# Maxima subtracted from attention scores: four matmuls of 512 columns a job in place of sixteen of 128

## The chip, the cores and the metric

The kernel runs on one core of a Trainium2 chip. The time is device time in microseconds (us) for one launch, as the median of several runs. The engines are named as in the profile: PE is TensorE's matmul array and PEld its weight loads, DVE is VectorE, ACT is ScalarE, POOL is GpSimd and SP is SyncE.

## The reference

Four transformer blocks work in turn on x (16 samples, 128 tokens, 128 channels). There are five attentions with 16 heads of 8 channels each: over the 128 tokens and then over the sample's context of 77 in the first block, over the context in the second, over the tokens and then the context in the third. The last block has one attention over the context without heads, then experts and a gate. What the change touches is the softmax of the attentions with heads. Cut to that:

```python
def mha(q, k, v):                      # q: 128 tokens, k and v: 128 or 77 tokens, 16 heads of 8
    scores = jnp.einsum('bqhd,bkhd->bhqk', qh, kh) / jnp.sqrt(d)
    attn = jax.nn.softmax(scores, axis=-1)
    out = jnp.einsum('bhqk,bkhd->bqhd', attn, vh)
    return out.reshape(B, Nq, C)
```

The softmax takes each row's maximum away before the exponential. The maximum belongs to a query and a head.

## The kernel before

The 16 samples go in four groups of four. An attention of one sample is a job; there are 5 x 16 = 80, numbered in the order in which they run. Each engine works through an order written out by hand (PE_ORDER, DVE_ORDER, ACT_ORDER, POOL_ORDER), and semaphores join them. In the orders, `s:j:g` is a score product of job j, `mx:j:g` its row maxima, `tu:j` and `tr:j` the turn of the maxima of jobs j and j+1, `st:j` the transposed score product, `su:j` the subtract, `ex:j:half` the exponentials, `av:j` the product with the values and `t1:j` its unloading.

The 128 channels lie on 128 partitions, so four strips of 32 partitions hold four heads each (strip g, head hh of the strip). A job runs as follows:

- `scores` (L1098, L1101, L1107, L1109): for each strip, queries on partitions and four heads' keys in a row of 512 or 308 columns, into one of the four banks of the PSUM tile ring. A bank is used by the next item but three, whatever it is, once the reader has freed it.
- `maximum` (L849, DVE): the maxima over the keys, four columns of mhl for each strip. Two jobs share one mhl: job j of a pair writes columns 32g + 4(j % 2) to +3.
- `turn` (L1145, PE, and L858, DVE), once for two jobs: mhl is transposed into a ring bank and copied to the tile mt, where row 32g + 4(j % 2) + hh has the maxima of that head by query.
- `scores_t` (L1128, L1133, L1137, PE): the same scores with the keys on partitions, into the PSUM tile big, one bank for each strip: 512 columns, four heads of 128 queries. It stays open for accumulation.
- `subtract` (L1154, PE): adds minus the maximum to each column of big. Each matmul works on one strip's 32 rows. The weights are a slice of indb, -1 in the row of the wanted head and job and 0 in the other 31 rows, for all kw key columns; the moving operand is the strip of mt, 128 columns. Four heads times four strips make 16 matmuls.
- ACT then takes the exponentials of big in two halves (L637, strips 0 and 1, then 2 and 3) into P, and frees big; PE multiplies P with the values (L1170).

On PE the subtract of an even job stands behind the turn in the order, often with `st` between (`tu:22 st:22 su:22`), at times with little or nothing (`tu:6 av:5 su:6`, `tu:20 s:22:1 su:20`). The subtract waits for the bank of the turn to be freed, which the copy L858 does. On DVE the copy stands among the row maxima of later jobs and among unloadings, as in `mx:22:0 tr:20 mx:22:1`.

The tile indb is made once at the start (`first_masks`): sel8 is summed from the identity, one column for each of the eight rows 4(j % 2) + hh that a strip uses, and indb is its negative, spread over 128 columns (L748).

Of the kernel before, what the change touches and what calls it, by code (L numbers as in the profile page):

```python
# [8 lines left out]
BF16 = mybir.dt.bfloat16  # L9
U8 = mybir.dt.uint8  # L10
ACT = mybir.ActivationFunctionType
ALU = mybir.AluOpType
AX = mybir.AxisListType.X

B, T, D, C = 16, 128, 128, 77
# [238 lines left out]
def job_of(j):  # L254
    return ORDER[j // GB] + (j % GB,)


def pair_of(j):

    return j - j % 2  # L260
# [25 lines left out]
def build(nc, x_in, ctx_in, ctxT_in, condT_in, ws_in, w_in, col_in, vcol_in, row_in, rw_in, rb_in, gb_in, mqk_in, mkq_in,  # L286
          mc_in, cos_in, sin_in, ident_in, ind_in, onesp_in, out):
    ctx = ExitStack()
    with ctx:
        def sb(name, shape, dt=F32):  # L290
            return ctx.enter_context(nc.sbuf_tensor(name, shape, dt))

        def ps(name, shape, dt=F32):
            return ctx.enter_context(nc.psum_tensor(name, shape, dt))
# [6 lines left out]
        big = ps("big", [128, 4, 512])  # L301
# [18 lines left out]
        oneb = sb("oneb", [128, 512], BF16)  # L320
        hm4 = sb("hm4", [128, 4])
        sel8 = sb("sel8", [128, 8])
        indb = sb("indb", [128, 8, 128], BF16)
        mqk8 = sb("mqk8", [128, 4, T], U8)
        mkq8 = sb("mkq8", [128, 4, T], U8)
        mc8 = sb("mc8", [128, B * C], U8)
# [42 lines left out]
        kbm = sb("kbm", [128, 2, 4, 128], BF16)  # L369
        P = sb("P", [128, 2, H, T])  # L370
        mhl = sb("mhl", [128, 2, 128], BF16)
        mt = sb("mt", [128, 2, 128], BF16)
        avt = [sb(f"avt{i}", [128, 2, GB * 128]) for i in range(2)]
        avm = [sb(f"avm{i}", [128, GB * 128]) for i in range(2)]
        rv = [sb(f"rv{i}", [128, 2, 16, 2]) for i in range(2)]
# [41 lines left out]
        def bank(item):  # L417
            return RING[item] % NB

        def full(eng, item):  # L420

            eng.wait_ge(ring_full[bank(item)], RING[item] // NB + 1)

        def taken(eng, item):

            eng.wait_ge(ring_free[bank(item)], RING[item] // NB + 1)

        def at(item, p=128):
            return ring[0:p, bank(item), :]

        def free(item):
            return ring_free[bank(item)]
# [267 lines left out]
        def _(dve):  # L700
            v = nc.vector
            n_setup = [0]

            def chain(i):
                n_setup[0] += 1
                i.then_inc(setup_dve, 1)
                dve.wait_ge(setup_dve, n_setup[0])
# [36 lines left out]
            def first_masks():  # L744
                dve.wait_ge(ident_ld, 16)
                v.tensor_copy(identb[:], ident[:])
                chain(v.tensor_reduce(sel8[:], ident[:].rearrange("p (g c) -> p c g", c=32)[:, 0:8, :], AX, ALU.add))
                v.tensor_scalar(indb[:], sel8[:].unsqueeze(2).broadcast_to([128, 8, 128]), -1.0, None, ALU.mult)  # L748
                dve.wait_ge(consts_in, 16 * 8)
                v.tensor_scalar(mqk[:], mqk8[:], -1.0, BIG, ALU.add, ALU.mult)  # L750
                v.tensor_scalar(mkq[:], mkq8[:], -1.0, BIG, ALU.add, ALU.mult).then_inc(masks_ready, 1)
# [30 lines left out]
            def statistics(k, s):  # L782
                t, o = (C, 1) if k == 4 else (128, 0)
                n, turn = s + NS * o, 1 if k == 4 else LN_TURN[k]
                src = ctx_t[s] if k == 4 else xs[s]
                if k == 4:
                    dve.wait_ge(ctx_in_s[s], 32)
                elif k == 0:
                    dve.wait_ge(x_in_s[s], 16)
                elif k in (5, 7):  # L790
                    taken(dve, ("o2" if k == 5 else "o4", "y", s))
                    hold(dve)
                else:
                    dve.wait_ge(x_ready[s], x_turn({1: "o0", 2: "o1", 3: "m0", 6: "o3", 8: "m1"}[k]))
                    hold(dve)
                for b in range(GB):
                    i = v.bn_stats(bst[s][0:t, o, b, :], src[0:t, b, :])
                i.then_inc(ln_bn[n], 1)
                dve.wait_ge(ln_bn[n], turn)
                for b in range(GB):  # L800
                    i = v.bn_aggr(mv[s][0:t, o, b, :], bst[s][0:t, o, b, :])  # L801
                i.then_inc(ln_stats[n], 1)
# [49 lines left out]
            def turn(j):  # L852
                item = ("tu", j)
                if j >= 4:

                    dve.wait_ge(st_full, 2 * (j - 3) + 2)
                full(dve, item)
                v.tensor_copy(mt[:, j // 2 % 2, :], at(item).bitcast(BF16)[:, 0:T]).then_inc(free(item), 1)  # L858

            def unload(j):  # L860
                item, p, b = ("av", j), j // GB, j % GB
# [102 lines left out]
            for item in DVE_ORDER:  # L964
                st, part, *_ = item
                if st == "mx":
                    maximum(part, item[2])
                elif st == "tr":
                    turn(part)
                elif st == "t1":  # L970
                    unload(part)
                elif st == "nr":
                    invert(part)
                elif st == "nt":
                    turn_back(part)
                elif st == "first":
                    (first_tables, first_weights, first_masks)[part]()
                elif st == "u":
                    unit(part)
                elif part == "stat":  # L980
                    statistics(int(st[1:]), item[2])
                elif part == "qc":
                    cast(int(st[1:]), item[2])
                elif st == "p0" and part in ("q", "k"):
                    roped(item[2], part)
                elif st == "p0" and part != "v":
                    rope(item[2], part)
                elif st[0] == "p":
                    values(int(st[1:]), item[2])
                elif st == "x3":  # L990
                    mixture(item[2], part)
                else:
                    add_result(st, item[2])

        @block.tensor
        def _(pe):
            mm = nc.tensor.matmul
# [10 lines left out]
            for c in range(2):  # L1008
                i = mm(big[:, 0, c * B:(c + 1) * B], WS[:, MODS[c][0], :], condT[:], start=True, stop=True)
# [137 lines left out]
            def subtract(j):  # L1147
                kw = ATT[job_of(j)[0]]["kw"]
                taken(pe, ("tu", pair_of(j)))
                for half in range(2):  # L1150
                    for hh in range(4):
                        for g in (2 * half, 2 * half + 1):
                            r = slice(32 * g, 32 * g + 32)
                            i = mm(big[0:kw, g, hh * T:(hh + 1) * T], indb[r, 4 * (j % 2) + hh, 0:kw], mt[r, j // 2 % 2, :], start=False,  # L1154
                                   stop=(hh == 3), skip_group_check=True)
                    i.then_inc(st_full, 1)

            def av(j):
# [142 lines left out]
            for item in PE_ORDER:  # L1301
                st, part, *_ = item
                if st == "s":
                    scores(part, item[2])
                elif st == "st":
                    scores_t(part)
                elif st == "tu":
                    turn(part)
                elif st == "su":
                    subtract(part)  # L1310
                elif st == "av":
                    av(part)
                elif st == "u":
                    unit(part)
                elif st == "f":
                    fold(part)
                elif part == "t":
                    norm(int(st[1:]), item[2])
                elif st[0] == "p":
                    project(int(st[1:]), item[2], part)  # L1320
                elif st[0] == "o":
                    outproj(int(st[1:]), item[2])
                elif st[0] == "m":
                    mlp(int(st[1:]), item[2], part)
                else:
                    mixture(item[2], part)
# [93 lines left out]
```

## Time and profile before

| | |
|---|---|
| median of 3 runs | 591.42 us (589.92 to 594.17) |
| the profiled execution | 592.24 us, its span 590.2 us |
| granted clock of TensorE in the profile, mean | 0.967 |
| PE busy | 553.6 us, 94% |
| DVE busy | 377.0 us, 64% |
| ACT busy | 311.6 us, 53% |
| POOL busy | 341.8 us, 58% |

The span is the time from the first to the last instruction; the time of the execution is longer by 2.0 us. Busy times are what an engine spent in instructions, overlaps counted once. A matmul that is recorded takes from its start to the arrival of its last column, and the next one starts before that; weight loads (PEld) overlap matmuls too. In the timeline, neighbours of one kind are merged into a row with the start of the first, the time until the end of the last and their number.

### The profile page before, as it was taken

What the parts mean: (1) busy time and instruction counts of PE and PEld (TensorE: products, weight loads), DVE (VectorE), ACT (ScalarE), POOL (GpSimd) and SP (SyncE); (2) the same over time, 40 slices, a digit from 0 to 9 for tenths busy, and PEclk for the clock granted to TensorE, in tenths of its full rate; (3) what the DMA queues carried; (4) which work ended last, traced back from release to release, by engine and by line L of the source; (5) the groups of instructions that cost most, each with busy time, mean ns of one, the idle gap of its engine ahead of it and who ended that gap; (6) DMA issues with size and microseconds to landing.
All of it is one profiled execution on the core that took longest, in us unless ns stands there. A gap on an engine that the chain in (4) does not pass through costs nothing. (4 is left out here: it accounts for less than half of the span.)

```text
span 590.2 us, 17700 instructions
## 1 busy us (share of the span) xinstructions
PE 553.6 (94%) x7235; PEld 346.6 (59%) x7260; DVE 377.0 (64%) x1034; ACT 311.6 (53%) x515; POOL 341.8 (58%) x428
## 2 busy tenths in 40 slices
PE   4899999899989999999999999999999999998996
PEld 1524455456545665566565655665577756866475
DVE  3567878975887468956795669888548404424024
ACT  1013365356445846766657565645846565535561
POOL 6365877486687768868746858779738103322000
PEclk8758999999999999999999999999999999998999
DMA  7800200000100010001000100000000000000000
GB/s 272 306 7 4 74 21 3 21 20 9 29 4 21 3 37 2 21 3 37 3 21 2 37 3 3 2 19 4 19 2 3 1 1 2 18 19 1 0 1 36
DMA packets 16574, 16.06 MB, mean 27 GB/s; under 512 B 3090, under 2 KB 14620, under 8 KB 16240
## 3 DMA queue, kind: packets, MB, share of 16 engines
q1 hardware_dynamic: 15632, 10.82, 6.0%
q10 hardware_dynamic: 864, 4.13, 1.8%
q8 instruction: 58, 0.95, 0.7%
q14 instruction: 20, 0.16, 0.1%
HBM read 13.85 MB, written 1.09 MB: 25 GB/s over the span
## 5 line engine op out<-in xcount | busy, mean ns | idle before, releaser
L637 ACT ACTIVATE P<-big 77x1024 f32<-77x1024 f32 (+1 forms) x160 | 155.2, 1018 | 130.9 <-PE big L1154 129.8
L849 DVE TENSOR_REDUCE mhl<-ring 128x4 bf16<-128x308 f32 (+1 forms) x320 | 164.4, 547 | 40.2 <-PE ring L1109 29.4
L564 POOL TENSOR_TENSOR qm<-qT,hm 128x512 f32<-128x512 f32 x80 | 85.1, 1068 | 36.6 <-PE big L1154 16.4
L536 POOL TENSOR_SCALAR xn<-x,mv,rstd 128x128 f32<-128x128 f32 x128 | 103.6, 821 | 3.3
L551 POOL TENSOR_TENSOR kbm<-kT,hm 128x308 bf16<-128x308 f32 (+1 forms) x80 | 68.5, 859 | 46.0 <-PE ring L1109 24.7
L1137 PE MATMUL big<-qm,kT 32*77 32x512 f32 (+1 forms) x640 | 92.1, 621 | 0.9 <-ACT P L637 0.8
L1029 PE MATMUL ring<-hT,W 128*128 128x512 f32 x176 | 91.9, 622 | 0.9 <-ACT hT L621 0.2
L1170 PE MATMUL ring<-P,Vp 77*32 77x128 f32 (+1 forms) x2560 | 86.6, 276 | 3.6 <-DVE mhl L849 1.4
L1170 PEld LDWEIGHTS ring<-P,Vp 77*32 77x32 f32 (+1 forms) x2560 | 65.4, 109 | 21.9 <-issue 13.1
L530 POOL TENSOR_SCALAR rstd<-mv 128x4 f32<-128x4 f32 (+1 forms) x36 | 9.7, 268 | 87.6 <-DVE mv L801 84.3
L621 ACT ACTIVATE hT<-ring,tab 128x128 f32<-128x128 f32 x96 | 35.9, 458 | 45.3 <-PE ring L1051 45.0
L1041 PEld LDWEIGHTS ring<-W,hid 128*128 128x128 f32 x480 | 57.4, 192 | 3.5 <-issue 2.6
L1041 PE MATMUL ring<-W,hid 128*128 128x128 f32 x480 | 57.5, 275 | 0.0
L1109 PE MATMUL ring<-kbm,qb 32*128 32x308 bf16 (+1 forms) x256 | 53.7, 317 | 3.6 <-issue 1.1
L1154 PEld LDWEIGHTS big<-mt,indb 32*77 32x77 bf16 (+1 forms) x1280 | 33.9, 104 | 31.7 <-issue 23.2
L866 DVE STREAM_TRANSPOSE avt<-ring 128x256 f32<-128x256 f32 x80 | 35.3, 442 | 21.6 <-PE ring L1170 20.8
L1029 PEld LDWEIGHTS ring<-hT,W 128*128 128x128 f32 x176 | 30.0, 193 | 29.1 <-issue 22.1
L670 ACT ACTIVATE hid<-ring,tab 128x128 f32<-128x128 f32 x112 | 31.4, 375 | 22.3 <-PE ring L1029 22.2
L532 POOL TENSOR_TENSOR rstd<-rstd,mhalf 128x4 f32<-128x4 f32 (+1 forms) x36 | 38.2, 1062 | 3.0
L1154 PE MATMUL big<-mt,indb 32*77 32x128 bf16 (+1 forms) x1280 | 39.2, 218 | 0.4
L575 POOL TENSOR_TENSOR avm<-avt,rv 128x256 f32<-128x256 f32 x40 | 24.5, 632 | 18.5 <-DVE rv L873 17.0
L1109 PEld LDWEIGHTS ring<-kbm,qb 32*128 32x128 bf16 x256 | 16.8, 92 | 28.5 <-issue 20.5
(164 smaller groups left out, 740.4 us busy)
## 6 DMA issues: line engine op xcount, KB each, us to landing
gring<-gate_rows SPq DMA_DIRECT2D x20, 256.0 KB, 3.4
W<-in_w ACTq DMA_DIRECT2D x1, 2624.0 KB, 14.4
hid<-in_ws SPq DMA_DIRECT2D x1, 1536.0 KB, 14.6
x<-in_x SPq DMA_DIRECT2D x4, 256.0 KB, 7.4
out<-x SPq DMA_DIRECT2D x4, 256.0 KB, 2.0
W<-in_w ACTq DMA_DIRECT2D x1, 768.0 KB, 4.8
ctxT<-in_ctxT SPq DMA_DIRECT2D x4, 154.0 KB
ctx<-in_ctx SPq DMA_DIRECT2D x4, 154.0 KB
```

The source lines that it names most:

```text
L532: nc.gpsimd.tensor_tensor(rstd[s][0:t, o, 1, :], rstd[s][0:t, o, 0, :], mhalf[0:t, :], ALU.pow).then_inc(ln_rstd[n], 1)
L536: i = nc.gpsimd.tensor_scalar(dst[0:t, b, :], src[0:t, b, :], mv[s][0:t, o, b, 0:1], rstd[s][0:t, o, 1, b:b + 1], ALU.subtract, ALU.mult)
L551: nc.gpsimd.tensor_tensor(kbm[:, j % 2, :, 0:kw], k.broadcast_to([128, 4, kw]), mask.broadcast_to([128, 4, kw]), ALU.mult).then_inc(kbm_re ...
L564: nc.gpsimd.tensor_tensor(qm[:, j % 2], q.broadcast_to([128, 4, T]), mask.broadcast_to([128, 4, T]), ALU.mult).then_inc(qm_ready, 1)
L637: nc.scalar.activation(P[0:kw, j % 2, 8 * half:8 * half + 8, :], big[0:kw, 2 * half:2 * half + 2, :].rearrange("p g (h q) -> p (g h) q", h=4),
L849: v.tensor_reduce(mhl[:, j // 2 % 2, c:c + 4], at(item)[:, 0:4 * kw].rearrange("p (h k) -> p h k", h=4), AX, ALU.max).then_inc(free(item), 1)
L1029: i = mm(at(item, m)[:, 0:n], w, a, start=(c == 0), stop=(c == len(parts) - 1))
L1041: i = mm(o[:, b * 128:(b + 1) * 128], a[:, b * t:(b + 1) * t], w, start=(c == 0 and bias is None), stop=(c == len(wts) - 1), skip_group_ch ...
L1109: give(item, mm(o, qb[s][r, b * T:(b + 1) * T], k_, start=(a > 1), stop=True, skip_group_check=True))
L1137: mm(big[0:kw, g, :].rearrange("p (h q) -> p h q", h=4), kT[s][r, b * kw:(b + 1) * kw], qm[r, j % 2], start=(a > 1), stop=False, skip_grou ...
L1154: i = mm(big[0:kw, g, hh * T:(hh + 1) * T], indb[r, 4 * (j % 2) + hh, 0:kw], mt[r, j // 2 % 2, :], start=False, stop=(hh == 3), skip_group ...
L1170: i_ = mm(at(item)[32 * g:32 * g + 32, i * T:(i + 1) * T], Vp[(j // GB) % 2][0:kw, b, h, :], P[0:kw, j % 2, h, :], start=(t == 0), stop=(t ...
```

## The change

The tile mt gets four times the columns: one part of 128 for each head hh, in which only the rows of head hh (of either job of the pair) have the maxima and all other rows are 0. DVE writes it with one multiply of the ring bank, read four times over, with head4, a column of ones and zeros for each head (`128 x 4`, spread over the queries). indb shrinks to one slice for each job of the pair, with -1 in that job's four rows of each strip. A subtract is then one matmul of 512 columns for each strip. In the setup, head4 and job2 are summed from sel8. The orders of all engines are as before, and so are the waits.

```diff
-        indb = sb("indb", [128, 8, 128], BF16)
+        indb = sb("indb", [128, 2, 128], BF16)
+        head4 = sb("head4", [128, 4])
+        job2 = sb("job2", [128, 2])
...
-        mt = sb("mt", [128, 2, 128], BF16)
+        mt = sb("mt", [128, 2, 4, T], BF16)
...
-                v.tensor_scalar(indb[:], sel8[:].unsqueeze(2).broadcast_to([128, 8, 128]), -1.0, None, ALU.mult)
+                v.tensor_tensor(head4[:], sel8[:, 0:4], sel8[:, 4:8], ALU.add)
+                chain(v.tensor_reduce(job2[:], sel8[:].rearrange("p (j h) -> p j h", j=2), AX, ALU.add))
+                v.tensor_scalar(indb[:], job2[:].unsqueeze(2).broadcast_to([128, 2, 128]), -1.0, None, ALU.mult)
...
-                v.tensor_copy(mt[:, j // 2 % 2, :], at(item).bitcast(BF16)[:, 0:T]).then_inc(free(item), 1)
+                v.tensor_tensor(mt[:, j // 2 % 2], at(item).bitcast(BF16)[:, 0:T].unsqueeze(1).broadcast_to([128, 4, T]),
+                                head4[:].unsqueeze(2).broadcast_to([128, 4, T]), ALU.mult).then_inc(free(item), 1)
...
                 for half in range(2):
-                    for hh in range(4):
-                        for g in (2 * half, 2 * half + 1):
-                            r = slice(32 * g, 32 * g + 32)
-                            i = mm(big[0:kw, g, hh * T:(hh + 1) * T], indb[r, 4 * (j % 2) + hh, 0:kw], mt[r, j // 2 % 2, :], start=False,
-                                   stop=(hh == 3), skip_group_check=True)
+                    for g in (2 * half, 2 * half + 1):
+                        r = slice(32 * g, 32 * g + 32)
+                        i = mm(big[0:kw, g, :].rearrange("p (h q) -> p h q", h=4), indb[r, j % 2, 0:kw], mt[r, j // 2 % 2],
+                               start=False, stop=True, skip_group_check=True)
                     i.then_inc(st_full, 1)
```

## Rows read from the trace of the kernel before

**Rows 1.** The page, part 1: busy time, share of the span, instructions.
```profile
PE 553.6 (94%) x7235; PEld 346.6 (59%) x7260; DVE 377.0 (64%) x1034; ACT 311.6 (53%) x515; POOL 341.8 (58%) x428
```
**Rows 2.** Waits, longest first: engine, line, releaser, us in total, times, longest.
```profile
ACT P L637 <- PE big L1154: 129.8, 63, 8.6
...
PEld big L1154 <- DVE mt L858: 5.2, 13, 0.9
...
PEld ring L1098 <- DVE mhl L849: 2.4, 3, 1.4
...
PEld ring L1041 <- DVE mhl L849: 1.8, 4, 1.1
```
**Rows 3.** Stages: start:end, length, busy us of PE, PEld, DVE, ACT, POOL; clock.
```profile
40.00:100.00 60.00, 56.51 (x922) 28.86 (x920) 46.50 (x117) 25.82 (x39) 43.13 (x52) 0.92 0.09 25
...
340.00:400.00 60.00, 56.84 (x978) 36.21 (x983) 50.49 (x128) 35.68 (x45) 43.98 (x53) 1.00 0.03 7
```
**Rows 4.** Groups by form (busy us, mean ns, idle before); the last: min/median/max ns.
```profile
L1109 PE MATMUL ring<-kbm,qb 32*128 32x308 bf16 x192 | 36.2, 296 | 1.6 <-issue 0.9 <-DVE mhl L849 0.7
L1109 PE MATMUL ring<-kbm,qb 32*128 32x512 bf16 x64 | 17.7, 382 | 2.0 <-POOL kbm L551 1.0 <-POOL qm L564 0.7 <-issue 0.3
L840 DVE CAST qb<-qT 128x512 bf16<-128x512 f32 x20 | 10.9, 543 | 10.4 <-ACT qT L607 10.0
L890 DVE TENSOR_TENSOR oT<-ring,gring 128x512 f32<-128x512 f32 x20 | 13.7, 687 | 18.7 <-PE ring L1041 18.7
L824 DVE TENSOR_TENSOR kT<-ring,cosT 128x512 f32<-128x512 f32 x4 | 2.8, 692 | 8.3 <-PE ring L1029 8.2
L858 DVE COPY mt<-ring 128x128 bf16<-128x128 bf16 x40 | 8.5, 212 | 11.6 <-PE ring L1145 11.4
L1154 PE MATMUL big<-mt,indb x1280: 212/214/309, 44.0 to 472.4; 32*77 32x128 bf16 x110, 32*128 32x128 bf16 x73
```
**Rows 5.** Timeline at a plain subtract, job 2: start, us, engine, line, operation.
```profile
55.86 1.14 PE L1137 MATMUL big<-qm,kT 32*128 32x512 f32 x8
56.82 0.41 PE L1154 MATMUL big<-mt,indb 32*128 32x128 bf16 x16
57.16 1.05 PE L1041 MATMUL ring<-W,hT 128*128 128x128 f32 x7
```
**Rows 6.** Timeline of PE where 512-column score matmuls precede a full-height item.
```profile
240.22 0.80 PE L1109 MATMUL ring<-kbm,qb 32*128 32x512 bf16 x3
240.95 0.54 PE L1170 MATMUL ring<-P,Vp 77*32 77x128 f32 x12
```
**Rows 7.** Stages, instructions of the tile mt alone (PE, PEld, DVE).
```profile
340.00:400.00 60.00, 7.81 (x240) 7.04 (x240) 1.51 (x7) 1.00 0.03 7
...
sum 440.00, PE 39.21 PEld 33.86 DVE 8.49; mean PE 4.90 PEld 4.23 DVE 1.06
```
**Rows 8.** Timeline of PE at a mixed subtract, job 40.
```profile
268.13 0.21 PE L1154 MATMUL big<-mt,indb 32*77 32x128 bf16 x1
...
268.58 0.26 PE L1154 MATMUL big<-mt,indb 32*77 32x128 bf16 x3
```
**Rows 9.** Timeline of a pair with margin, jobs 24 and 25.
```profile
178.62 0.23 DVE L858 COPY mt<-ring 128x128 bf16<-128x128 bf16 x1 [0.73 <-PE ring L1145]
...
180.16 0.41 PE L1154 MATMUL big<-mt,indb 32*128 32x128 bf16 x16
```
**Rows 10.** Timeline of a pair without margin, jobs 20 and 21.
```profile
162.98 0.22 DVE L858 COPY mt<-ring 128x128 bf16<-128x128 bf16 x1
...
163.25 0.29 PEld L1154 LDWEIGHTS big<-mt,indb 32*77 32x77 bf16 x16 [0.36 <-DVE mt L858]
```
**Rows 11.** Timeline where a score product waits for a row maximum.
```profile
117.04 0.10 PEld L1098 LDWEIGHTS ring<-mqk,identb 32*32 32x32 bf16 x4 [0.73 <-DVE mhl L849]
```
**Rows 12.** Timeline of DVE in the setup.
```profile
8.30 0.69 DVE L748 TENSOR_SCALAR indb<-sel 128x1024 bf16<-128x1024 f32 x1
11.79 0.43 DVE L750 TENSOR_SCALAR mqk<-mqk 128x512 bf16<-128x512 uint8 x1 [2.80 <-DMA mkq<-in_mkq]
```

## The prediction

> **What bounds the kernel now.** I read the busy times first. The array (PE) is busy for 553.6 of 590.2 us, 94%; VectorE (DVE) for 377.0, 64% [rows 1]. PE's own waits are short: the longest in total are a few microseconds, and none of the larger ones is at the subtract (L1154) [rows 2]. So the order of the array's work sets the time, and the change is worth what it takes from the array's path or puts on it. By stage the picture holds: PE is busy for 56.5 of 60 us between 40 and 100 and for 56.8 between 340 and 400, VectorE for 46.5 and 50.5; the second of these is its fullest stage [rows 3]. ScalarE waits for the subtract for 129.8 us in all, in 63 pieces [rows 2]. That is no bottleneck, but it says that whatever makes a subtract late makes ScalarE's exponentials late as well.
>
> **Part 1, the matmuls.** A job's subtract is 16 matmuls of 128 columns now and 4 of 512 after: the same columns. What matters is how long the array is held. A single 128-column matmul has 0.214 us [rows 4], yet all 16 together take 0.41 us from the first start to the last end, and the next item, a full-height projection, starts 0.34 us after the first of them [rows 5]. The 16 starts thus lie within 0.41 - 0.214 = 0.20 us. What a column costs comes from L1109: its 512-column form takes 382 ns and its 308-column form 296 ns, so 86 ns for 204 columns, 0.42 ns each [rows 4]. 128 columns are then 0.054 us of streaming and 512 are 0.215. Sixteen starts in 0.20 us are three steps of 0.054 between four groups of four: the four strips of 32 rows already work side by side, although the program names strips 0 and 1 in the first half and 2 and 3 in the second. The strips hold 4 x 0.054 = 0.215 us each, and four matmuls of 512 columns, one in each strip, hold them for 0.215 as well. The streaming gains nothing.
>
> What of the hand-over to the next item? After the last 128-column start (57.02) the next item starts at 57.16, so 0.14 us, of which 0.054 is streaming and 0.09 a gap [rows 5]. After the last of three 512-column matmuls with 32 rows (240.22 + 0.80 - 0.39 = 240.63) a full-height item starts at 240.95, 0.32 us, of which 0.215 is streaming and 0.10 the same gap [rows 6]. After the change: some 0.02 for four starts, plus 0.32, makes 0.34, against 0.34 before. A plain subtract gains 0.
>
> Not all are plain. The busy time of the subtract's matmuls is 39.21 us over the eight stages that hold all 80 jobs [rows 7], 0.49 us a job, against 0.41 for the plain one. In the others score matmuls (L1107, L1109) come between: at 268.13 the 16 run until 268.84, some 0.71 us, with several score matmuls among them [rows 8]. Most of that is the scores' own streaming in the same strip, which stays. Upper bound of the gain: all of it goes, 80 x (0.49 - 0.40) = 7 us, 0.40 being one 512-column matmul of 0.382 plus the spread of 0.02. Lower bound: 0. I take **2 us gained**, nearer to the plain case, since about 0.06 us in each of some thirty mixed jobs can be weight loads left uncovered between the small matmuls. The 960 weight loads that go lie under matmuls in the plain case and are counted in this.
>
> A rule of the Trainium skill speaks for a larger gain. The page "TensorE: Matmul & The Clock Gate", section "Part 3: Packing small matmuls — row/col tiling", says that matmuls start and end in strict program order, whatever strip they use. By that rule strips 2 and 3 could start only after the first half, the 16 would need about 8 steps and the change would save about 0.2 us a job. The trace does not agree: 16 starts in 0.20 us leave no room for eight steps of 0.054 [rows 5].
>
> **Part 2, the tile on VectorE.** The copy of 128x128 to mt (L858), 0.212 us on average [rows 4], becomes a multiply of 128x512 from the ring bank with the head mask. It isn't in the trace. The nearest rows are the multiplies of 128x512 from the ring with a tile in SBUF: L890 at 687 ns and L824 at 692 ns; a cast of 512 elements within SBUF takes 543 ns [rows 4]. I take 0.69 (the same operation from the same memory), the cast as the low bound. So a turn costs 0.48 us more, 40 x 0.48 = 19 us of VectorE's time in all. Two places must be priced: who waits for mt, and who waits for what is queued behind it on VectorE.
>
> Who waits for mt: the subtract of the even job of each pair, on PE, with everything queued behind it there. I went through the 40 pairs in the timeline and took, for each, the time from the end of the copy to the first subtract matmul, less the 0.055 us that the signal takes at the shortest. In 27 pairs the margin is over 0.48 us, because the large score product (L1137, 0.96 us from its first start to the subtract [rows 5]) or more lies between: a copy ends at 178.85 and its subtract starts at 180.16 [rows 9]. In 13 it is less, from nothing (the copy ends at 163.20, the subtract starts at 163.25 [rows 10]) up to 0.46. The list of waits has the same number: 13 waits of the subtract's weight load for the copy, 5.2 us in all [rows 2]. The margins of the 13 add up to 2.0 us, so the loss is 13 x 0.48 - 2.0 = **4.2 us**. The odd jobs use the same mt a whole job later and have margin.
>
> Who waits for what is behind it: the row maxima (L849), which free the ring banks that PE takes next. PE waits for them today for a few microseconds in all: 2.4 + 1.8 us are the largest entries [rows 2]. At 117.04, for one, a score product starts 0.73 us late because of a maximum [rows 11]. Where VectorE then has a gap, the 0.48 us vanish in it; where it runs through, they are handed on. Bounds: 0, and one delay of 0.48 for each of the 27 pairs that don't already wait, 13 us. Following VectorE from each copy to its next gaps, and looking who takes a freed bank within the delay, I find some ten places with 0.3 us each. I take **3 us**. The odd price, the wait of L858 for its own ring item, does not change.
>
> **Part 3, the setup.** indb is written with 256 elements in place of 1024 (L748, 0.69 us) and two small operations are added. Behind them VectorE waits 2.80 us for the masks to arrive [rows 12]. That wait is the cover for either sign: 0. Without it the part would gain at most half a microsecond.
>
> **Sum**, against the profiled execution of 592.24 us (span 590.2 and 2.0 around it): -2 + 4.2 + 3 = +5.2 us. Not all of a stall on PE reaches the end: PE idles for 36.6 us of its span, places where a delay can be lost. That is 6%, and the idle places stand where the chains cross, so I keep about four fifths, **+4 us: 596**. The median of the runs shown is 591.42, 0.8 us below the profiled one. I stay on the profiled scale and forecast 596, with 592 to 600 as this case's own range.
>
> **Rivals.** (a) *VectorE becomes the bound of its full stretches.* In 340 to 400 us seven turns [rows 7] add 3.4 us to 50.49 of 60 [rows 3]. If VectorE's queue is what PE follows there and in like stretches, the delays don't die in gaps. It decides from the point where a pair's idle time on VectorE is under 0.48. Price at its worst: 4.2 + 13 lost and 0 to 2 gained, so 607 to 609; in part, from 600 up. For it: 84% busy there. Against it: PE's waits for VectorE are small today. (b) *The longer tile is covered.* Only the bare waits (the 8 pairs of the 13 with under 0.15 us of margin, 0.4 us together) grow, by 8 x 0.48 - 0.4 = 3.4 us, the banks cost nothing, and the mixed jobs give back 3: 592.6. The wait list speaks for it, the fullness of VectorE against it. (c) *The array does gain.* Either the two halves run one after the other, 4 x 0.054 = 0.2 us saved in each of 80 jobs, 16 us less (chance 0.03), or the mixed jobs give the full 7 and the gap before the next item closes because its weights load under the long matmuls, 80 x 0.09 = 7 more (chance 0.07). With the 7 of losses: 592.2 + 7 - 14 to 16, 583 to 585.5. Against it: [rows 5] for the first, and [rows 6] for the second, where the gap stands after 512 columns too. The first of the two is what the order rule of the Trainium skill's page named above would give. (d) *The change does nothing* but swap equal work, with neither stalls nor gains: also 592, and taken with (b).
>
> **How the numbers follow.** Forecast (592 to 600) 0.48; (a) 0.22; (b) with (d) (588 to 592.5) 0.20; (c) 0.10. The range leaves out the worst half of (a) and (c): 587 to 603. A difference of 1%, 5.9 us, is about what a measurement of this kernel can tell from none; against 591.4 it is reached at 597.3 and at 585.5. The forecast's upper third and all of (a) lie above: 0.16 + 0.20 = 0.36 slower; faster 0.10; same 0.54.
>
> **What the profile of the changed kernel would show.** The new multiply at about 0.69 us x40. The subtract's four matmuls within some 0.4 us and the next full-height item 0.34 us after the first: if 0.25 or less, the gap closed and (c) has a part. PE's waits for mt up from 5.2 us to about 10, in more pairs than 13. Waits of PE for L849 up by some 3 us; if by over 8, (a). PE's busy time nearly unchanged. The prediction is wrong if the multiply takes under 0.4 us, if a plain subtract holds the array for clearly less than 0.34, or if VectorE's delay is passed on in the full stretches.

## The result and the profile after

| | before | changed |
|---|---|---|
| median of the runs | 593.22 us (588.32 to 597.23, 20 runs) | 597.59 us (591.39 to 601.16, 20 runs) |
| the profiled execution | 592.24 us, span 590.2 | 591.71 us, span 589.6 |
| granted clock in it, mean | 0.967 | 0.982 |

The changed kernel is slower: the ratio of the times is 1.0065, with a 95% interval from 1.0038 to 1.0092. (Ratios leave out executions over 1.5% above the fastest of the same kernel, like the 601.16 here; medians and ranges hold them all.) Yet its profiled execution is 0.5 us *shorter* than the one of before. This has to be cleared up first. The page of the changed kernel, part 1:

```profile
PE 548.4 (93%) x6275; PEld 326.1 (55%) x6300; DVE 391.9 (66%) x1036; ACT 312.4 (53%) x515; POOL 341.5 (58%) x428
```

The stages at the start, of before (start:end, length, busy us of PE, PEld, DVE, ACT, POOL, clock):

```profile
26.20:33.00 6.80, 4.77 (x54) 2.11 (x55) 5.30 (x37) 0.00 (x0) 6.59 (x8) 0.50 0.41 110
33.00:50.00 17.00, 15.54 (x125) 3.75 (x124) 9.74 (x17) 4.72 (x7) 7.44 (x9) 0.50 0.00 1
```

The same of the changed kernel:

```profile
26.10:32.90 6.80, 5.08 (x55) 2.31 (x56) 5.31 (x37) 0.00 (x0) 6.49 (x8) 0.50 0.42 118
32.90:50.00 17.10, 16.10 (x218) 6.04 (x221) 14.88 (x31) 6.67 (x9) 11.03 (x13) 1.00 0.01 2
```

In both executions the granted clock is at its lower level (0.50, 1.2 GHz) around 26 to 33 us. In the one of before it stays there until 50; in the other it is back at the upper level (2.4 GHz) from 32.9. In the same 17 us the array gets through 218 matmuls in place of 125. That the change did not make this difference is seen from a second profile of the changed kernel ("changed, again" below). There the clock was low from 24.5 to 31.3 us and once more in this stage:

```profile
34.70:48.40 13.70, 12.62 (x102) 3.09 (x94) 8.53 (x14) 1.94 (x2) 5.42 (x7) 0.50 0.01 1
```

Its subtract of job 5 starts at 73.3 us, as in before (73.9), and not at 68.4 as in the first profile of the same kernel. So a profiled execution starts with a head start or a handicap of several microseconds. The 20 runs of the changed kernel have mean clocks from 0.961 to 0.982, and the six that are at 0.982, like the profiled one, took 591.4 to 592.8 us, the others 595.6 to 601.2.

The change has to be read from a stretch without such a piece. I take the one from the first subtract matmul of job 5 to that of job 77. It has its ends at the same work in every kernel. Differences are taken from the starts of these matmuls; the stages below have the same ends rounded to 0.1 us. Before:

```profile
73.90:455.40 381.50, 366.11 (x5739) 228.65 (x5755) 283.55 (x737) 226.79 (x320) 275.34 (x342) 1.00 0.05 13
```

The same stretch of the changed kernel:

```profile
68.40:454.70 386.30, 366.31 (x4875) 211.50 (x4891) 297.22 (x737) 227.47 (x320) 275.43 (x342) 1.00 0.05 13
```

The clock is 1.00 throughout in both. The stretch takes **4.8 us more** (386.3 - 381.5), about 0.8% of the whole, which is what the ratio of the runs says. PE's busy time in it is the same within 0.2 us, though this sum is only good to some microseconds: a kernel below with before's matmuls has 22 records more of them in this stretch. So the array does as much work as before and stands longer. VectorE is busy 13.7 us longer. The stretch starts at 73.9 and at 68.4: these 5.5 us, which lie in the clock at the start, covered the loss in the profile.

The parts. Groups of instructions (busy us, mean ns, idle before), the subtract's matmuls of before first, then two of the changed kernel:

```profile
L1154 PE MATMUL big<-mt,indb 32*77 32x128 bf16 (+1 forms) x1280 | 39.2, 218 | 0.4
L1160 PE MATMUL big<-mt,indb 32*77 32x512 bf16 (+1 forms) x320 | 39.1, 380 | 3.3 <-DVE mt L864 3.2
L864 DVE TENSOR_TENSOR mt<-ring,head 128x512 bf16<-128x512 bf16 x40 | 27.2, 680 | 11.6 <-PE ring L1152 11.4
```

The changed kernel's list of waits:

```profile
ACT P L639 <- PE big L1160: 125.8, 64, 5.2
PEld big L1160 <- DVE mt L864: 13.8, 20, 1.6
PEld ring L1116 <- DVE mhl L854: 3.4, 9, 0.9
PEld ring L1116 <- DVE mt L864: 1.0, 3, 0.4
```

Its timeline at a plain subtract, job 4, and at the pair of jobs 20 and 21:

```profile
64.61 0.39 PE L1160 MATMUL big<-mt,indb 32*128 32x512 bf16 x4
64.93 0.38 PE L1048 MATMUL ring<-W,oT 128*128 128x128 f32 x1
...
157.89 0.69 DVE L864 TENSOR_TENSOR mt<-ring,head 128x512 bf16<-128x512 bf16 x1
158.50 0.47 DVE L854 TENSOR_REDUCE mhl<-ring 128x4 bf16<-128x308 f32 x1
158.64 0.12 PEld L1160 LDWEIGHTS big<-mt,indb 32*77 32x77 bf16 x4 [0.83 <-DVE mt L864]
```

Four matmuls of 512 columns hold the array for 0.32 us until the next full-height item, where sixteen of 128 held it for 0.34 [rows 5]. The busy time of the subtract's matmuls is 39.1 us as it was [rows 7]. The multiply takes 0.680 us in place of 0.212 [rows 4]. At jobs 20 and 21 the array stands until the multiply ends (157.89 + 0.69 = 158.58, first weight load at 158.64), as it did for the copy [rows 10]. The subtract's weight loads now wait for mt 20 times and for 13.8 us, where it was 13 times and 5.2 [rows 2]. The array itself idles 3.3 us before the subtract's matmuls, 3.2 of it for mt, where it was 0.4 in all. Waits for row maxima grow as well, over all lines: those of the weight loads from 7.8 to 10.6 us, those of the array from 5.9 to 7.1. And three score products now wait for the multiply, 1.0 us together; before had no such wait.

### The profile page after: what moved, and what is told of

The parts are those of the page before. It is cut to its first block and busy times, and to the rows that moved or that the text cites. A ratio compares the mean times of both kernels' runs of the same rounds, so it can differ in the third digit from the quotient of the medians.

```text
span 589.6 us, 15782 instructions
## 1 busy us (share of the span) xinstructions
PE 548.4 (93%) x6275; PEld 326.1 (55%) x6300; DVE 391.9 (66%) x1036; ACT 312.4 (53%) x515; POOL 341.5 (58%) x428
## 5 line engine op out<-in xcount | busy, mean ns | idle before, releaser
L1160 PE MATMUL big<-mt,indb 32*77 32x512 bf16 (+1 forms) x320 | 39.1, 380 | 3.3 <-DVE mt L864 3.2
L577 POOL TENSOR_TENSOR avm<-avt,rv 128x256 f32<-128x256 f32 x40 | 24.5, 632 | 20.6 <-DVE rv L880 19.0
L1116 PEld LDWEIGHTS ring<-kbm,qb 32*128 32x128 bf16 x256 | 17.1, 92 | 33.6 <-issue 22.7
L864 DVE TENSOR_TENSOR mt<-ring,head 128x512 bf16<-128x512 bf16 x40 | 27.2, 680 | 11.6 <-PE ring L1152 11.4
## 6 DMA issues: line engine op xcount, KB each, us to landing
W<-in_w ACTq DMA_DIRECT2D x1, 2624.0 KB, 14.9
```

Source lines behind the costliest of these rows:

```text
L1116: give(item, mm(o, qb[s][r, b * T:(b + 1) * T], k_, start=(a > 1), stop=True, skip_group_check=True))
L1160: i = mm(big[0:kw, g, :].rearrange("p (h q) -> p h q", h=4), indb[r, j % 2, 0:kw], mt[r, j // 2 % 2], start=False, stop=True, skip_group_c ...
```

## The experiments

Each kernel was timed beside the kernel before on the same chip. Since the clock pieces move whole runs by several microseconds, the table also has the stretch from job 5 to job 77, and the later part of it from job 41 to 77, each as the difference to before (381.5 and 182.2 us). "Clock" is what pieces at the lower level the stretch held.

| kernel | ratio, 95% interval | 5 to 77 | 41 to 77 | clock |
|---|---|---|---|---|
| changed kernel | 1.0065 [1.0038, 1.0092] | +4.8 | +2.0 | none |
| changed, again | 1.0135 [1.0088, 1.0182] | +4.8 | +2.0 | none |
| wide tile alone | 1.0180 [1.0129, 1.0231] | +7.4 | +3.6 | none |
| four matmuls alone | 0.9983 [0.9952, 1.0014] | -1.4 | -1.2 | none |
| delay behind the copy, multiply | 1.0258 [1.0210, 1.0306] | +13.3 | +3.3 | 17.1 us |
| delay behind the copy, reduce | 1.0076 [1.0041, 1.0112] | +3.8 | +1.9 | none |
| changed, subtracts later | 1.0167 [1.0112, 1.0222] | +18.9 | +2.0 | 2 x 17.1 us |
| before, subtracts later | 1.0139 [1.0071, 1.0206] | +10.5 | 0.0 | 17.1 us |
| two heads at a time | 1.0051 [1.0016, 1.0087] | +0.3 | -0.1 | none |
| multiply twice | 1.0463 [1.0418, 1.0508] | +30.5 | +12.0 | 6.8 and 3.4 us |
| half-wide tile alone | 1.0036 [0.9979, 1.0093] | +3.1 | +0.9 | 3.4 us |
| before, three subtracts later | 1.0039 [0.9989, 1.0089] | +3.1 | +0.2 | 2 x 3.4 us |

The second line is the changed kernel once more, timed together with the next three kernels. Its ratio is twice as far from 1 as the first one, and the two intervals barely touch, while its stretch is the same within 0.03 us. Before with nine or with three subtracts later has before's own time from job 45 to job 77 (within 0.04 us of 164.2), too. For differences under 1% the stretch is therefore the better evidence. It leaves out what happens outside it: the kernel with two heads at a time is 0.5% slower by its runs and the same by the stretch.

The expectations count to job 79 (398.3 us before). I end at job 77, because in three kernels (wide tile alone, delay with the reduce, three subtracts later) a short piece at the lower clock lies between the two. Where an expectation names a time, the time to job 79 is given beside it.

> The changed kernel itself, for its time on the same chip as the three others: 3 to 6 us slower than before, and 403 us between the subtracts of jobs 5 and 79.

To job 79 it took 403.1 us, as expected; its runs were 7.5 us above before's, not 3 to 6 (597.46 us, 592.68 to 599.93, 6 runs, beside 589.97).

### The wide tile alone

```diff
+                    for hh in range(4):
+                        for g in (2 * half, 2 * half + 1):
+                            r = slice(32 * g, 32 * g + 32)
+                            i = mm(big[0:kw, g, hh * T:(hh + 1) * T], indb[r, j % 2, 0:kw], mt[r, j // 2 % 2, hh, :], start=False,
+                                   stop=(hh == 3), skip_group_check=True)
```

> VectorE's part of the change alone: mt is written 512 columns wide by the multiply with the head mask, and the subtract stays at 16 matmuls of 128 columns. My theory puts the whole loss here: the turn is 0.47 us longer, the 13 bare subtracts and the freed banks cost 4 to 7 us against before, and the run is as slow as the changed kernel or up to 2 us slower; between the first plain subtract of a full-clock stretch (job 5) and the last (job 79), 398.3 us before, it takes 403 to 405. The rival, that four wide matmuls cost the array something of their own, expects this run at before's time.

It ran in 599.73 us (597.73 to 646.14, 6 runs) beside 589.97. Its stages for the stretch, and its waits:

```profile
69.20:458.10 388.90, 369.00 (x5742) 228.07 (x5759) 297.99 (x737) 227.53 (x320) 276.24 (x342) 1.00 0.05 13
```
```profile
PEld big L1161 <- DVE mt L864: 13.4, 20, 1.4
```

388.9 - 381.5 = 7.4 us lost: the wide tile costs more than the whole change. To job 79 it is 406.4 us, more than the 403 to 405 expected. The waits for mt are those of the changed kernel, and the array's own idle time for mt is 2.8 us. The change's matmuls beside this tile are worth 4.8 - 7.4 = -2.6 us.

### The four matmuls alone

Each strip's matmul reads the 128 columns of the copied mt four times over, with the weights of one head. It adds a wrong head's maximum to three quarters of the scores, and the exponentials get a smaller scale so that they stay finite; the work is otherwise that of before.

```diff
+                        i = mm(big[0:kw, g, :].rearrange("p (h q) -> p h q", h=4), indb[r, 4 * (j % 2), 0:kw],
+                               mt[r, j // 2 % 2, :].unsqueeze(1).broadcast_to([32, 4, T]), start=False, stop=True,
+                               skip_group_check=True)
```

> TensorE's part alone: mt is copied 128 columns wide as before, and the subtract is four matmuls of 512 columns that read mt's strip four times over. The computation differs in two places: all four heads of a strip get the maxima of the first one, and the exponential is scaled down by 0.001 so that nothing overflows. My theory: 16 small matmuls already ran four side by side, so 0 to 3 us are gained against before, and a plain subtract is followed by the next full-height item after 0.32 us against 0.34. The rival (the array gains by fewer matmuls) expects 7 to 16 us less.

It ran in 588.96 us (585.19 to 594.18, 12 runs). Stages for the stretch, waits, and the timeline at a plain subtract:

```profile
71.40:451.60 380.20, 363.89 (x4876) 211.85 (x4891) 283.64 (x737) 227.11 (x320) 276.28 (x342) 1.00 0.05 13
```
```profile
PEld big L1153 <- DVE mt L858: 5.9, 13, 0.9
```
```profile
67.64 0.39 PE L1153 MATMUL big<-mt,indb 32*128 32x512 bf16 x4
67.96 1.16 PE L1041 MATMUL ring<-W,oT 128*128 128x128 f32 x8
```

The starts of the matmuls are 380.1 us apart, against 381.5: 1.4 us gained, over 72 jobs 0.02 us each, which is the difference of the plain case (0.32 against 0.34). The waits for mt stay at 13. So the array gains little, whatever VectorE does.

### The delay behind the copy alone

To tell those who wait for mt from those who wait for what is queued behind it, the copy stays as it was, and an idle operation stands behind it. mt is ready as before; VectorE is later for the rest. First with a multiply of 312 columns:

```diff
+        pad = sb("pad", [128, 312])
...
                 v.tensor_copy(mt[:, j // 2 % 2, :], at(item).bitcast(BF16)[:, 0:T]).then_inc(free(item), 1)
+                v.tensor_tensor(pad[:].rearrange("p (a b) -> p a b", a=3), onesf[:, 0:104].unsqueeze(1).broadcast_to([128, 3, 104]),
+                                onesf[:, 0:104].unsqueeze(1).broadcast_to([128, 3, 104]), ALU.mult)
```

> The kernel before with an idle operation of 312 elements (about 0.48 us) on VectorE right behind the copy to mt, so that mt and the ring bank are ready as early as before and only what is queued behind is late. It separates the two prices of the longer turn. By the sum of the prediction: 3 us slower than before, with PE's waits for the copy as before (13, about 5 us). The rival, that the delay of the queue is the main price, expects 5 us or more; a rival by which it dies in gaps expects 0 to 1.

It ran in 605.4 us (601.37 to 610.48, 6 runs). It does not measure the queue alone. Its idle operation took 0.626 us on average (statistics of its line below, min/median/max), and the clock was at 0.50 from 102.5 to 119.6:

```profile
L860 DVE TENSOR_TENSOR pad<-onesf x40: 458/474/1349, 40.6 to 469.7; 128x312 f32<-128x312 f32 x40
```

What stretched the operation stands in the trace. The longest one, with GpSimd's operations around it:

```profile
181.57 1.04 POOL L565 TENSOR_TENSOR qm<-qT,hm 128x512 f32<-128x512 f32 x1
181.60 1.35 DVE L860 TENSOR_TENSOR pad<-onesf 128x312 f32<-128x312 f32 x1
182.57 1.28 POOL L552 TENSOR_TENSOR kbm<-kT,hm 128x512 bf16<-128x512 f32 x1
```

It ends at 182.95, 0.34 us after the qm that was running when it started (181.57 + 1.04 = 182.61). Of the 14 idle operations over 0.6 us, 12 start while a two-operand operation of GpSimd (qm, kbm or avm) is running, and each of the 12 ends 0.33 to 0.35 us after it. All that ran with GpSimd idle took 0.46 to 0.47. The kbm that starts inside it takes 1.28 us, where the same one takes 1.04 in the run with the reduce below. So this delay is longer than meant in 14 places, and it delays GpSimd too.

The 13.3 us divide at job 17: 6.5 up to there, with the piece at the lower clock, and 6.8 from there to job 77 with the clock at 1.00, as much as the wide tile costs in that part (6.7). They are not the price of a queue that is 0.47 us late. The delay was repeated with a reduce of one operand:

```diff
+        pad = sb("pad", [128, 3])
...
+                v.tensor_reduce(pad[:], onesf[:, 0:104].unsqueeze(1).broadcast_to([128, 3, 104]), AX, ALU.max)
```

> The kernel before with an idle reduction over 312 elements of one SBUF tile (about 0.47 us, one operand) behind the copy to mt. In the earlier run of this kind the idle operation read SBUF twice and took 0.63 us on average, up to 1.35, so it overstated the delay. If the queue's price is 3 us as in the prediction's sum, the stretch between the subtracts of jobs 5 and 79 takes 401 to 402 us; if the queue is the main price of the wide tile (8.1 us in that stretch in all), 404 or more; if it dies in gaps, 398 to 399.

596.97 us (593.48 to 598.27, 10 runs). Stages for the stretch, waits, and the timeline of VectorE around the turn of jobs 20 and 21:

```profile
69.20:454.50 385.30, 372.10 (x5761) 229.00 (x5756) 294.93 (x773) 227.23 (x320) 275.14 (x342) 1.00 0.05 13
```
```profile
PEld big L1156 <- DVE mt L859: 6.3, 15, 0.9
PEld ring L1111 <- DVE mhl L850: 2.7, 7, 0.9
```
```profile
158.50 0.22 DVE L859 COPY mt<-ring 128x128 bf16<-128x128 bf16 x1
158.64 0.47 DVE L860 TENSOR_REDUCE pad<-onesf 128x3 f32<-128x312 f32 x1
159.03 0.85 DVE L850 TENSOR_REDUCE mhl<-ring 128x4 bf16<-128x308 f32 x2
```

385.3 - 381.5 = 3.8 us lost, with the waits for mt nearly as before, and with no idle time of the array for mt. To job 79 it is 402.6 us, between the 401 to 402 of the prediction's sum and the 404 of its rival. So about half of the wide tile's price is the queue behind it. The delay is slightly smaller than the tile's: here the next row maximum starts 0.53 us after the copy's start (158.50 to 159.03), of which the copy's own share is 0.14 (to 158.64); in the changed kernel it starts 0.61 after the multiply's (157.89 to 158.50). In proportion (0.61 - 0.14 = 0.47 to 0.53 - 0.14 = 0.39) the queue's part would be up to 4.6 us, an estimate. What is left of the 7.4 is 2.8 to 3.6. This is a difference of two runs: it holds the waits for mt, the three waits of a score product for the multiply, and whatever the two prices do to each other.

### Covering the waits: subtracts later in PE's order

In nine jobs whose subtract stands bare behind the turn, the subtract and the item behind it change places, in the changed kernel and in the one before.

```diff
+LATER = (6, 10, 20, 22, 28, 30, 36, 46, 62)
+for _j in LATER:
+    _k = PE_ORDER.index(("su", _j))
+    PE_ORDER[_k], PE_ORDER[_k + 1] = PE_ORDER[_k + 1], PE_ORDER[_k]
```

> The changed kernel with the subtracts of jobs 6, 10, 20, 22, 28, 30, 36, 46 and 62 one item later in PE's order, so that the longer turn of these pairs is covered. If the bare waits for mt cost 4 us, some 3 of them come back and the stretch from job 5 to 79 takes 400 to 401 us in place of 403.1; if the main price lies in the queue, it stays at 402.5 to 403.5.

> The same nine subtracts one item later in the kernel before. There the copy costs 0.21 us and seven of the nine are bare or nearly so, with 0.2 to 0.9 us of standing each: 1 to 2 us less than before in the stretch (396.5 to 397.5) if that standing is real, no change if it is only moved on to ScalarE's exponentials.

Both were slower than what they started from: 602.47 us (596.3 to 603.76, 6 runs) and 600.7 (595.85 to 604.85, 6 runs), to job 79 417.2 and 408.8 us. The waits for mt did shrink. In the changed kernel with the swaps, and in before with them:

```profile
PEld big L1165 <- DVE mt L869: 7.3, 14, 0.8
```
```profile
PEld big L1159 <- DVE mt L863: 2.1, 7, 0.4
```

13.8 us became 7.3, and 5.2 became 2.1. From job 41 on, where the clock is at 1.00 and jobs 46 and 62 have moved, nothing is gained all the same: +2.0 with or without the swaps in the changed kernel, 0.0 in before. The next score products stand behind the row maxima of the same VectorE queue. I read this as the stall only changing its name; no run takes both waits away at once.

The loss is early. In before with the swaps 1.4 us are gone by job 17, at the upper clock throughout, where the subtracts of jobs 6 and 10 have moved. The timeline at job 22 and the stages after it:

```profile
173.21 0.44 PE L1159 MATMUL big<-mt,indb 32*77 32x128 bf16 x16
...
173.78 1.04 POOL L569 TENSOR_TENSOR qm<-qT,hm 128x512 f32<-128x512 f32 x1 [1.17 <-PE big L1159]
174.77 1.04 POOL L556 TENSOR_TENSOR kbm<-kT,hm 128x512 bf16<-128x512 f32 x1
...
175.87 0.60 PE L1103 MATMUL ring<-mqk,identb 32*32 32x512 bf16 x4 [1.41 <-POOL kbm L556]
```
```profile
175.90:193.00 17.10, 17.10 (x205) 10.31 (x205) 7.75 (x21) 4.96 (x8) 6.30 (x8) 0.50 0.06 18
```

GpSimd's next qm waited 1.17 us for the later subtract, and kbm stands behind it in GpSimd's order. PE in turn waited 1.41 us for kbm, and right behind that wait the clock is at 0.50 for 17.1 us, with PE busy all the time. From job 17 to job 26, which holds both the wait and this piece, 7.6 us are lost; another 1.3 go between jobs 26 and 32, at the upper clock. The changed kernel with the swaps has the same piece at 176.1, and another of 17.1 us at 101.0; the other eleven profiles have none between 123 and 282 us. So the piece comes with the swaps. That the wait of 1.41 us brought it is likely, but no run takes away that wait alone.

The last three swaps alone (jobs 36, 46 and 62), on before:

> The kernel before with only the subtracts of jobs 36, 46 and 62 one item later. In the run with nine moved ones the clock fell at 175.9 us, after an idle stretch behind the moved subtract of job 22; this leaves that out. If the bare waits for mt are worth their length, the stretch is 0.3 to 0.7 us shorter than before; if the banks that the same VectorE queue frees are the next thing late, it is unchanged within 0.1.

595.19 us (590.84 to 596.72, 8 runs), ratio 1.0039, to job 79 402.1 us. From job 45 to 77, where jobs 46 and 62 have moved, the difference is 0.0: nothing is gained. Of the 3.1 us that its stretch lost, 2.7 lie before job 17, where its order is still that of before. There it has two pieces of 3.4 us at the lower clock, at 103.9 and 117.6, which no swap explains.

### How the price grows with the turn

Three kernels change the length of the turn. The half-wide tile has two copies of the maxima (heads of even and of odd number) and takes 0.412 us; in the first kernel eight matmuls of 256 columns use it, in the second the sixteen of before. The third writes the wide tile twice, once to a buffer that nobody reads.

```diff
-        mt = sb("mt", [128, 2, 4, T], BF16)
+        mt = sb("mt", [128, 2, 2, T], BF16)
...
+                    for m in range(2):
...
+                            i = mm(big[0:kw, g, 256 * m:256 * m + 256].rearrange("p (h q) -> p h q", h=2), indb[r, 2 * (j % 2) + m, 0:kw],
+                                   mt[r, j // 2 % 2], start=False, stop=(m == 1), skip_group_check=True)
```

> Half the change: mt 256 columns wide (two masks, by the parity of the head) and eight matmuls of 256. The multiply should take about 0.42 us (0.21 more than the copy, against 0.47 for the full change). My theory has the loss grow with the length of the turn and only part of the pairs exposed: 8.1 us for 0.47 more would be 2.5 to 3.5 for 0.21, less about 1 gained on the array, so 400 to 401 us in the stretch. The rival, that any multiply in place of the copy costs the same, expects 403.

594.11 us (590.58 to 598.73, 12 runs). Groups and waits:

```profile
L864 DVE TENSOR_TENSOR mt<-ring,head 128x256 bf16<-128x256 bf16 x40 | 16.5, 412 | 12.1 <-PE ring L1152 11.9
```
```profile
PEld big L1161 <- DVE mt L864: 8.5, 16, 1.3
```

The stretch differs from before by +0.3 us (398.6 us to job 79, where 400 to 401 was expected): the matmuls' gain and the tile's price cancel.

```diff
+                v.tensor_tensor(mt2[:], at(item).bitcast(BF16)[:, 0:T].unsqueeze(1).broadcast_to([128, 4, T]),
+                                head4[:].unsqueeze(2).broadcast_to([128, 4, T]), ALU.mult)
```

> As the run with the wide tile alone (16 matmuls of 128), but the multiply is done twice, first into a spare tile: the turn takes about 1.3 us in place of 0.68. If the price of a longer turn rises as the margins run out (most of the 27 covered pairs have 0.5 to 1.4 us), the stretch from job 5 to job 77 costs over 20 us more than before; if it is proportional (7.4 us for 0.47), 17 to 18.

619.64 us (2 runs) beside 592.95; to job 79 429.3 us, 31 more than before, of which up to 5 can be the two pieces at half clock. Its waits:

```profile
PEld big L1164 <- DVE mt L867: 28.0, 25, 2.0
PE big L1164 <- DVE mt L867: 12.5, 19, 1.2
```

The half-wide tile with the sixteen matmuls:

> The half-wide tile alone: mt 256 columns, the subtract at 16 matmuls of 128. The turn is 0.20 us longer than the copy. Proportional to the full width it costs 3.1 us in the stretch from job 5 to 77; if the margins of most pairs swallow it, 1 to 2.

595.94 us (591.24 to 598.02, 6 runs). The stretch lost 3.1 us, but it holds a piece at half clock from 118.8 to 122.2. From job 41 on there is none, so this part is the better one to compare. There the price of the tile, with sixteen matmuls throughout, is 0.9 us for a turn longer by 0.20 us, 3.6 for 0.47, and 12.0 for 1.15 (2 x 0.68 less the copy's 0.21). With 18 pairs in this part that is 0.05, 0.20 and 0.67 us for each pair: about a quarter, two fifths and three fifths of the delay. A short delay mostly vanishes in margins; of a longer one, a growing share reaches the end. The rival by which any multiply in place of the copy costs the same is refuted by it.

## Why the prediction was right

The direction and the size were right: 596 forecast from 592.24, that is +0.6%, and +0.65% measured, with the stretch at +4.8 us against a sum of +5.2. The two losses, 7.2 us in the sum, are 7.4 in the wide tile alone. By its own steps:

- **The strips work side by side.** The plain subtract was priced at 0.34 us after as before; it is 0.32. The four matmuls alone gain 1.4 us in the stretch, forecast 2. Beside the wide tile they are worth 2.6, which was not foreseen; the runs don't show why the two parts don't simply add.
- **The strict order.** If the halves of a subtract had to run one after the other, 16 us would have gone. The four matmuls alone gave 1.4, so that part of rival (c) is refuted for this pattern, as the trace of before had said [rows 5]. The same trace shows the order too: the matmul that signals the end of a subtract's first half is the eighth in the program, and in 57 of the 80 jobs it is the fourteenth of the sixteen to start. The gap before the next item did not close either.
- **The multiply.** 0.69 us from L890 [rows 4], 0.680 measured. VectorE's busy time rose by 14.9 us, not 19. The multiplies are longer than the copies by 18.7 together (27.2 - 8.5), so the rest lies in how VectorE's operations overlap elsewhere and wasn't traced further; the overlap of 0.08 us behind the multiply (158.50 to 158.58) was there behind the copy too.
- **Those who wait for mt.** Forecast 4.2 us; 2.8 to 3.6 by difference (the wide tile alone less the delay behind the copy). The array's own idle time for mt agrees: 3.2 us in the changed kernel, 2.8 in the wide tile alone, none in before. The list of waits rose more than I wrote, to 13.8 us in 20 pieces and not to about 10. That entry of the list counts only weight loads and takes their whole idle time, of which PE's matmuls in flight cover some. The sum had the other waits for this operation at nothing: three score products lose 1.0 us to it.
- **The queue behind.** Forecast 3 us, measured 3.8, up to 4.6 in proportion. The list agrees: the waits for row maxima rose by 2.8 us before weight loads and 1.2 on the array, where "some 3" was the sign. This was the term with the widest bounds (0 to 13), and the way it was found, following VectorE from each copy to its next gap, held. The price (a) of 13 us didn't come.
- **The fifth that is lost.** I took four fifths of the sum. The stretch kept 4.8 of the 5.2, and the two losses without the gain came out whole (7.4 of 7.2), so the discount had no ground that the runs show; that it brought the forecast near the ratio of the runs is luck.
- **The setup.** Priced at nothing. The clock falls at 26.2 us before and at 26.1 after, so nothing of weight shows up to there. VectorE waits 3.13 us for the masks in place of 2.80 [rows 12]: indb is done sooner and the wait takes it up, as forecast. It wasn't measured alone.
- **What was missing.** The clock at the start. I set the forecast on the scale of one profiled execution, taking its whole span for comparable. The stretch begins 5.5 us apart in the two executions, more than the change is worth. Compared by its span, the profile of the changed kernel would have called the change a gain.

My expectations of the swaps failed, and for a reason that bears on the prediction: I had counted the waits for mt and the queue as two prices that can be removed one by one. Without the first, the second is next, as I read it.

What stays open: why five kernels show pieces at the lower clock between 101 and 123 us, some of them (the half-wide tile, the three late swaps) though little or nothing is changed before them; why the swaps of jobs 6 and 10 cost 1.4 us; and how the wide tile's price divides exactly between its two parts.

## What to carry to other kernels

Ask first whether small matmuls in different strips already overlap: if their starts lie closer than their streaming time in one strip allows, merging them gains next to nothing, and no gain on the array pays for a wider tile that another engine must write for them. To price a longer operation on an engine that is not the bottleneck, count the places where its result is awaited bare and those where the next item of its queue is; covering only the first gained nothing here. A forecast of this kind can be made pair by pair from the trace: count each margin, and expect that a delay longer than the margins costs more than in proportion. Compare two kernels by a stretch between two pieces of the same work in which the granted clock is equal, before comparing spans.

## What the runs showed of the hardware

- Sixteen 128-column matmuls, four in each strip, take as long as four of 512 but for 0.02 us (0.34 and 0.32 us to the next item), although in the program strips 2 and 3 come after all of strips 0 and 1. In 57 of the 80 subtracts of before, the matmul that is eighth in the program is the fourteenth to start. The Trainium skill, page "TensorE: Matmul & The Clock Gate", "Part 3: Packing small matmuls — row/col tiling", says that matmuls start and end in strict program order; the measurement differs and decides here.
- An operation of VectorE with two operands in SBUF had a median of 0.474 us and single ones up to 1.349, while a one-operand reduce of the same 312 elements stayed between 0.449 and 0.469 at all 40 places. In 12 of the 14 cases over 0.6 us a two-operand operation of GpSimd was running at its start, and it ended 0.33 to 0.35 us after that one; with GpSimd idle it took 0.46 to 0.47.
- A wait of 1.41 us on the array was followed by 17.1 us at the lower clock, and the nine jobs around the two (17 to 26) lost 7.6 us. Both kernels with the nine swaps have this piece and no other kernel has it there.
